# Scores of an attention layer on four row tiles: a head's 96 stacked rows cut into three pieces of 32

## The reference

```python
qkv = x @ Wqkv                                   # 16 heads of 16 features
q, k = apply_rope(q), apply_rope(k)
q = q / jnp.sqrt(jnp.sum(q * q, -1, keepdims=True) + 1e-06)   # k likewise
attn = jax.nn.softmax(jnp.einsum('bthd,bshd->bhts', q, k) / math.sqrt(HD), axis=-1)
out = jnp.einsum('bhts,bshd->bthd', attn, v).reshape(b, t, d) @ Wo + bo
x = _layernorm(x + out)
```

## Time and profile before

| what | us |
|---|---|
| median of 3 runs | 1380.87 |
| the profiled execution | 1376.04 |
| its span, first to last instruction | 1374.0 |
| TensorE busy / ScalarE busy / VectorE busy in the span | 1256.9 / 915.8 / 793.3 |

### The profile page before, as it was taken

One profiled execution on the slowest core, in us unless ns is written; L12 is line 12 of the kernel. 1 busy time (PEld: TensorE's weight loads), 2 busy tenths in 40 slices (PEclk: granted clock), 3 DMA queues, 4 the chain that ended last, 5 costly groups with the idle time before them and its releaser, 6 DMA issues. The chain is left out here.

```text
span 1374.0 us, 20853 instructions
## 1 busy us (share of the span) xinstructions
PE 1256.9 (91%) x7142; PEld 674.2 (49%) x7142; DVE 793.3 (58%) x1815; ACT 915.8 (67%) x1617; POOL 323.5 (24%) x246
## 2 busy tenths in 40 slices
PE   4699999999998898999999999999982899999996
PEld 2233343343343333444444444444332799999986
DVE  5236456456451777787878787878744234443432
ACT  1588878878876575676766666666661477776765
POOL 3113332332331111022222222222123012212211
PEclk8899999999999899999999999999996899999998
DMA  5173243243243121214131313131349211111110
GB/s 180 64 170 105 72 139 98 71 141 95 73 137 108 47 90 50 79 47 109 47 109 47 109 47 109 48 93 47 126 153 311 71 56 51 54 56 51 58 52 15
DMA packets 101485, 123.11 MB, mean 90 GB/s; under 512 B 7234, under 2 KB 87234, under 8 KB 101379
## 3 DMA queue, kind: packets, MB, share of 16 engines
q1 hardware_dynamic: 76534, 83.35, 19.6%
q10 hardware_dynamic: 20416, 25.56, 5.9%
q0 software_dynamic: 4432, 12.87, 3.1%
HBM read 47.41 MB, written 24.27 MB: 52 GB/s over the span
## 5 line engine op out<-in xcount | busy, mean ns | idle before, releaser
L692 ACT ACTIVATE w_space<-bank 128x512 f32<-128x512 f32 x1024 | 561.7, 606 | 277.7 <-PE bank L472 263.6
L886 DVE TENSOR_REDUCE negm<-bank 128x1 f32<-128x512 f32 x512 | 334.3, 685 | 97.9 <-PE bank L504 94.4
L472 PE MATMUL bank<-w_space 96*128 96x512 bf16 (+1 forms) x1024 | 355.1, 385 | 26.5 <-DMA w_space<-work_space 14.2
L489 PE MATMUL bank<-w_space 128*32 128x512 f32 x2048 | 275.3, 610 | 0.2 <-ACT w_space L701 0.2
L472 PEld LDWEIGHTS bank<-w_space 96*128 96x128 bf16 (+1 forms) x1024 | 93.5, 99 | 303.7 <-ACT w_space L692 217.3
L504 PE MATMUL bank<-w_space 96*128 96x512 bf16 x512 | 197.5, 386 | 18.1 <-DVE negm L886 8.8
L666 PE MATMUL bank<-w_space,work_space 128*128 x624 | 141.2, 380 | 0.0
L535 PE MATMUL bank<-work_space,wqkv_sb 128*128 128x512 f32 x256 | 125.0, 613 | 9.5 <-DMA wqkv_sb<-in_w_qkv_dram 6.4
L1245 POOL TENSOR_TENSOR work_space<-w_space,work_space 128x1024 bf16<-128x1024 f32 x32 | 68.3, 2133 | 266.3 <-ACT work_space L742 146.5
L666 PEld LDWEIGHTS bank<-w_space,work_space 128*128 128x128 f32 x624 | 115.6, 190 | 14.3
L1300 POOL DMA_INDIRECT out_dram<-rows_sb,work_space x39 | 59.8, 1533 | 241.9 <-DVE rows_sb L1197 241.9
(11 more groups left out here) (130 smaller groups left out, 1414.3 us busy)
## 6 DMA issues: line engine op xcount, KB each, us to landing
w_space<-work_space SPq DMA_DIRECT2D x372, 128.0 KB
w_space<-in_w_dram SPq DMA_DIRECT2D x10, 1024.0 KB, 14.2
work_space<-rows_dram SPq DMA_DIRECT2D x39, 256.5 KB, 2.6
w_space<-in_w_dram ACTq DMA_DIRECT2D x6, 1024.0 KB, 6.3
work_space<-in_x_t_dram ACTq DMA_DIRECT2D x8, 512.0 KB, 3.7
work_space<-in_x_dram ACTq DMA_DIRECT2D x8, 512.0 KB
x_dram<-xo SPq DMA_DIRECT2D x16, 256.0 KB, 4.2
h_dram<-row_sb SPq DMA_DIRECT2D x16, 256.0 KB, 2.2
```

Source lines behind the costliest of these rows:

```text
L472: nc.tensor.matmul(bank[:, :], k_stack[0:rows, b % 2, HEADS_AT_ONCE * g + j, kt * P:(kt + 1) * P], q_stack[0:rows, b % 2, HEADS_AT_ONCE * ...
L489: last = nc.tensor.matmul(pv_bank[VW * j:VW * (j + 1), :], v_aug[:, b % 2, at:at + VW], probs[:, q % PROBS, j, :], start=(kt == 0), stop=( ...
L692: nc.scalar.activation(probs[:, q % PROBS, j, :], st_bank(b, c)[0][:, :], ACT.Exp, scale=SCALE).then_inc(exps, 1)
L886: ve.tensor_reduce(negm[:, c % TT, c // TT:c // TT + 1], mx_ring.bank(b, (g, c))[:, :], axis=AX.X, op=ALU.max, negate=True).then_inc(mx_ri ...
```

## The change

In the first layer the stack of a head becomes three pieces of 32 rows. The 32 rows of head j of a group lie on partitions 32j to 32j + 31, so four heads fill 128 partitions, and piece `part` of group g stands at place 4g + part of the free dimension. `score_quad` makes the scores of all four heads at the head of a quad (chunk 0): three passes, in each one matmul of 32 rows per head, the four heads on four row tiles and into four banks, and the three passes add up in the bank. The first pass of each head waits for its bank; each head's last pass counts its score. The weights' columns, the rotation tables and the matrix that sums squares are laid out so that the stack's DMAs (same number and bytes) write 32 partitions x 4 places in place of 8 partitions x 16 places.

Scores of the first layer use five banks (0 to 3 and 7) until quad 10 of batch 7 (`ALL_BANKS`), then three; there the fourth head waits for the first head's exponential and goes alone. `o_ring` keeps bank 5 alone. The row of ones moves from the first loads to two loads on SP behind the k copies of units 8 and 9, as the first layer now uses all partitions. Some tasks of the first layer move: on VectorE aq, ak, uk, hk and lk (ak now after hq), on TensorE nk by one chunk, and on ScalarE sq, sk, nq, nk, TP0, TP1, R1 and R2 to places behind the fourth exponential of a quad, the copy of oT too (`COPY_AFTER` 3). The second layer's scores are made as before.

```diff
+ALL_BANKS = CHUNKS * LAST_A + HEADS_AT_ONCE * (QUADS - MAX_LEAD)
...
-    dict(qA=(0, 3), qB=(1, 2), kA=(2, 3), kB=(3, 3), sq=(3, 3), aq=(4, 3), nq=(6, 0), sk=(6, 1),
-         uq=(7, 1), ak=(7, 2), hq=(7, 2), lq=(8, 0), nk=(8, 2), uk=(9, 2), hk=(9, 3), lk=(10, 1),
+    dict(qA=(0, 3), qB=(1, 2), kA=(2, 3), kB=(3, 3), sq=(3, 3), aq=(5, 0), nq=(6, 0), sk=(6, 1),
+         uq=(7, 1), hq=(7, 2), ak=(8, 0), lq=(8, 0), nk=(8, 3), uk=(10, 1), hk=(10, 2), lk=(11, 0),
...
-ACT_LAG = (dict(other=1),
+ACT_LAG = (dict(sq=4, nq=3, sk=6, nk=4, TP0=3, TP1=4, R1=2, R2=2, other=1),
...
-COPY_AFTER = (1, 2)
+COPY_AFTER = (3, 2)
...
-        st_banks, mx_banks, pv_bank = psum[0:4], (psum[3], psum[7]), psum[6]
+        st_banks, mx_banks, pv_bank = psum[0:4] + psum[7:8], (psum[3], psum[7]), psum[6]
...
-        o_ring = Ring("out", [psum[5], psum[7]], sem)
+        o_ring = Ring("out", [psum[5]], sem)
...
-            if b < LAST_A:
-                return st_banks[c % 4], CHUNKS * b + c - 3
-            return st_banks[(CHUNKS * (b - LAST_A) + c) % 3], CHUNKS * b + c - 2
+            n = CHUNKS * b + c
+            if n < ALL_BANKS:
+                return st_banks[n % 5], n - 4
+            return st_banks[(n - ALL_BANKS) % 3], n - 2
...
+        def slot_of(stack, b, slot, half):
+
+            at = 2 * slot + half
+            if second(b):
+                return stack[at:STACK:ROW_STEP, b % 2, :, :]
+            return stack[at % 4:P:4, b % 2, slot // 2:H:4, :]
...
+            def score_quad(b, q):
+
+                g, kt = q // TT, q % TT
+                if q == 0:
+                    for arrived in stack_in:
+                        pe.wait_ge(arrived, 16 * STACK_DMAS * (b + 1))
+                own = [st_bank(b, HEADS_AT_ONCE * q + j) for j in range(HEADS_AT_ONCE)]
+                banks = len({id(bank) for bank, _ in own})
+                for heads in (range(banks), range(banks, HEADS_AT_ONCE)):
+                    for part in range(3):
+                        at = 4 * g + part
+                        for j in heads:
+                            bank, read = own[j]
+                            if part == 0:
+                                wait(pe, exps, read)
+                            rows = slice(32 * j, 32 * j + 32)
+                            last = nc.tensor.matmul(bank[:, :],
+                                                    k_stack[rows, b % 2, at, kt * P:(kt + 1) * P],
+                                                    q_stack[rows, b % 2, at, :],
+                                                    start=(part == 0), stop=(part == 2))
+                            if part == 2:
+                                last.then_inc(scores, 1)
...
-                        pe.wait_ge(exps, CHUNKS * LAST_A)
-                        pe.wait_ge(o_ring.drained[1], o_ring.used[1])
+                        pe.wait_ge(exps, ALL_BANKS)
...
-                        if attended is not None:
+                        if attended is not None and second(attended):
                             score(attended, HEADS_AT_ONCE * q + j)
+                        elif attended is not None and j == 0:
+                            score_quad(attended, q)
...
-                (w1_space[STACK:STACK + NEG, H * T:2 * H * T], ones_pairs))
...
+                    if qk and b in (BATCH, BATCH + 1):
+                        at = H * T + b % 2 * (H * T // 2)
+                        sp.dma_start(w1_space[STACK:STACK + NEG, at:at + H * T // 2],
+                                     ones_pairs[:, 0:H * T // 2]).then_inc(ones_in, 16)
```

More of the change, by code:

```diff
@@ L318, in program @@
         neg_in = sem("neg_in")
+        ones_in = sem("ones_in")
         x_in = [sem("x_in0"), sem("x_in1")]
@@ L347, in program @@
         h_out = [sem("h_out0"), sem("h_out1")]
[L348 to L351 removed]
+        N_FIRST, N_LATER, N_CONST_OPS = 5, 12, 3
+        st_banks, mx_banks, pv_bank = psum[0:4] + psum[7:8], (psum[3], psum[7]), psum[6]
         p_ring = Ring("proj", [psum[i] for i in (4, 0, 1, 2, 3, 5, 6, 7)], sem)
[L353 removed]
+        o_ring = Ring("out", [psum[5]], sem)
         mx_ring = Ring("max", mx_banks, sem)
@@ L361, in program @@
                         elif name[:2] in OUT_BANK:
-                            o_ring.add(b, name, len(o_ring.uses) % 2 if n <= LAST_A else 0)
+                            o_ring.add(b, name, 0)
         for b in range(BATCH, 2 * BATCH):
@@ L440, in stack_copies @@
                     for half in range(2 if slots[slot] == part else 0):
-                        eng.dma_start(stack[2 * slot + half:STACK:ROW_STEP, b % 2, :, :],
+                        eng.dma_start(slot_of(stack, b, slot, half),
                                       parts[:, qk, part, half, :]).then_inc(stack_in[qk], 16)
@@ L467, in score @@
                         pe.wait_ge(arrived, 16 * STACK_DMAS * (b + 1))
+                if second(b) and c == 0:
+                    pe.wait_ge(ones_in, 16 * min(b - BATCH + 1, 2))
                 if second(b) and j == 0 and kt == 0:
@@ L1326, in _ @@
                 (gate_w_sb[:, 0, :], gate_w[0:P, :]), (gate_w_sb[:, 1, :], gate_w[P:D, :]),
-                (gate_b_sb[:, :], gate_b.partition_broadcast(P)),
-                (w1_space[STACK:STACK + NEG, H * T:2 * H * T], ones_pairs))
+                (gate_b_sb[:, :], gate_b.partition_broadcast(P)))
             assert (len(first), len(later)) == (N_FIRST, N_LATER)
@@ L1387, in lay_out, with columns @@
     a = {k.removeprefix("L0_"): np.asarray(v) for k, v in inputs.items()}
-    def columns(w):
-        qk = w[:, :2 * D].reshape(D, 2, H, 2, HALF).transpose(0, 1, 3, 4, 2).reshape(D, 2 * D)
+    def columns(w, second):
+        qk = w[:, :2 * D].reshape(D, 2, GROUPS, HEADS_AT_ONCE, 2, HALF)
+        qk = qk.transpose((0, 1, 4, 5, 2, 3) if second else (0, 1, 4, 3, 5, 2)).reshape(D, 2 * D)
         return np.ascontiguousarray(np.concatenate([qk, w[:, 2 * D:]], axis=1))
@@ L1393, in lay_out @@
     angles = (np.arange(T, dtype=np.float32)[None, :] * inv_freq.astype(np.float32)[:, None])
-    table = lambda f: np.repeat(f(angles).astype(np.float32), H, axis=0)
-    of_head = np.arange(P) % H
+    head_rows = np.arange(P).reshape(HEADS_AT_ONCE, HALF, GROUPS)
+    of_half = ((head_rows // GROUPS) % HALF).reshape(P)
+    table = lambda f: f(angles).astype(np.float32)[of_half]
+    of_head = (head_rows % GROUPS * HEADS_AT_ONCE + head_rows // (P // HEADS_AT_ONCE)).reshape(P)
     return {
-        "x": a["attn_x"], "x_t": a["attn_x"].transpose(0, 2, 1), "w_qkv1": columns(a["attn_Wqkv"]), "w_o1": a["attn_Wo"],
+        "x": a["attn_x"], "x_t": a["attn_x"].transpose(0, 2, 1), "w_qkv1": columns(a["attn_Wqkv"], False), "w_o1": a["attn_Wo"],
         "b_o": a["attn_bo"], "ln1_w": a["ffn_ln1_w"], "ln1_b": a["ffn_ln1_b"],
-        "w_qkv2": columns(a["ffn_w_qkv"]), "w_o2": a["ffn_w_proj"], "ln2_w": a["ffn_ln2_w"],
+        "w_qkv2": columns(a["ffn_w_qkv"], True), "w_o2": a["ffn_w_proj"], "ln2_w": a["ffn_ln2_w"],
         "ln2_b": a["ffn_ln2_b"], "gate_w": a["ffn_gate_w"], "gate_b": a["ffn_gate_b"],
```

## The result

The changed kernel takes **1395.18 us** (median of 4 runs, 1393.39 to 1395.96); the kernel before took 1380.36 beside it on the same chip. The ratio is 1.0107, with a 95% interval of 1.0095 to 1.0119: slower by 1.1%, 2 us from the forecast. The profiled execution took 1395.14 (span 1393.2).

A forecast was written before the change was run, and what follows sets the result against it. TensorE was taken as the bound (busy 50.05 of a 51.37 us stage), ScalarE some 10 behind. Stages +7.4, start +1.5 and batch 7 +3 made +11.9 us: 1387.9 from the profiled execution, 1393 on the median; range 1367 to 1410.

The forecast's parts named there:

- long quads: First-layer quads with an output projection: from 3.70 to 3.60 us each, eight of them giving back 0.8 a stage.
- Scores: A quad's scores: four matmuls of 0.22 (0.88) become three rounds taken at 0.72, lower end 0.65, upper end 1.16.
- The rival that weights don't overlap: Weight loads run one behind the other: a quad's scores take 1.16, not 0.72, kernel 1442 us; chance 0.06.
- Drains: Each change between row tiles, column tiles and full width costs 0.09; 15 extra a stage, 1.35 us.
- The fourth head: Head 3 waits for the previous quad's third exponential: quad 13 +0.56, quads 11 and 15 together +0.24.
- the prediction's signs: What would show it right, including TensorE waiting for exponentials at the head of quads 5, 6, 13 and 15.
- Quads 4 to 8: ScalarE has no hole, TO0 waits for TP1's copy in the one out bank: 15.79 against 14.63, +1.16.
- A stage: One steady first-layer stage: -0.80 + 0.56 + 0.24 + 1.16, less about 0.1, so +1.05; seven stages +7.4 us.
- Start: Before the first score: hq's four operations now stand ahead of the k sum, bounds 0 and 2, taken +1.5 us.
- nothing, if they land as fast: k copies cost nothing if 32 partitions land as fast as 8; otherwise lateness falls on the next stage's first score.
- Batch 7: Last six quads have three banks, head 3 waits and runs alone: +1.34 each, 8.0 at most, taken +3 us.
- The clock rival: Two standstills a stage could halve the clock for 3.4 us over quad 8: +1.5 a stage, 1403 us; chance 0.04.

The follow-up runs named there:

- order2: Changed kernel with TP0 and TP1 moved to quads 3 and 4 and the k half normalised a quad sooner: 1384.17 us, ratio 1.0049.
- order3: order2 with VectorE adding k's squares ahead of TO0's division: 1382.38 us, ratio 1.0030.
- order5: order3 with VectorE splitting the k half behind the sum of WO0 instead of ahead of it: 1377.39 us, ratio 1.0002.

## Why the prediction was right

The forecast (slower, 1393) held, and so did the mechanism of the stages: TensorE waits for ScalarE in quads 4 to 8 and 14, and long quads gain next to nothing. The stage's loss was twice what the sum has, though, the start had the wrong sign and batch 8 was left out, and that the total came out 2 us off is in good part luck.

- **Scores.** Rounds start 0.226 and 0.216 apart (records of quad 10: 287.162, 287.388, 287.604); with the drain 0.76, where 0.72 + 0.09 was taken: the lower end. The rival that weights don't overlap is out by the 0.34 for twelve loads.
- **Drains: the step that was mis-sized.** A change between row and column tiles costs 0.10 (0.66 + 0.10 = 0.76), near the 0.09 taken. A projection behind the product with v costs more: 1.92 up to the next score, where 1.73 + 0.09 = 1.82 was forecast. The first two of L615's eight matmuls stand 0.320 apart, the others 0.216. I read the 0.10 as a full-width load (0.19) that nothing hides: the first two loads start only 0.108 apart, the second ends 0.03 ahead of the second matmul, and every later one lies under the matmul ahead of it. Before, a score stood between product and projection, the loads started with it, and the first two matmuls stood 0.220 apart. So the seven long quads other than quad 14 gave back 0.04 in all (forecast 0.7). The Trainium skill (TensorEngine Tiling (Array Packing), Key Properties) has a change of tiling mode drain TensorE; the trace agrees, at 0.09 to 0.10 a change.
- **The fourth head.** Quads 13 and 14 together went from 5.66 to 6.15, +0.49; forecast 0.56 - 0.10. The wait stands at the head of quad 14, not of 13 as the prediction's signs have it, since it is the quad behind a short one that waits. Quads 11 and 15 together grew by 0.09, not 0.24: quad 11 shrank by 0.06, and the 0.15 of quad 15 come from ScalarE's wait for VectorE shown above (2.34 in order2).
- **Quads 4 to 8.** The mechanism as told: TP1's copy at 12.03 after the start of quad 4 (forecast 11.86), TO0 at 12.71 (12.53), the end at 16.11 (15.79): +1.48 for +1.16. TensorE stood 1.63 longer over quad 6's scores and 1.64 ahead of TO0.
- **A stage** so comes to +2.03, not +1.05: 0.66 of the difference comes from the seven long quads (0.13 of it a wait of quad 12's fourth head, the rest mainly the loads behind drains), 0.32 from quads 4 to 8; the other terms cancel. The k copies cost nothing, as forecast: no first score of these stages waits for a DMA.
- **Start: wrong in sign.** -3.2 for +1.5. The first score came at 40.87, not 44.06, its wait for the copies 7.88 instead of 14.22. The copies of both kernels begin at 25.3. From their first packet to the end of the last they take 15.1 with row tiles in nine of the ten profiles (13.8 with the old order) and 17.9 to 18.5 in the four profiles of the layout of before, under either order. So the 32-partition copies land sooner; "nothing, if they land as fast" left out that they could be faster.
- **Batch 7** +2.2 for +3, but the clock is in it (0.91 before, 0.93 after), so that the term was right isn't shown. **Batch 8** was no term: +4.9. Of that 1.72 lies in its quads 5 and 7 and comes with the order (0.49 and 1.23 also in the run with the new order alone; the 1.23 is gone where TP1's copy comes earlier), and 3.2 in the quads with the two stretches at half clock shown above, which the kernel before doesn't have. In the 10 us ahead of the one at 539.60 TensorE never stood for more than 0.94. Why the grant fell there stays open.
- **The clock rival** didn't come in this kernel, whose standstills were 1.6; it did in batches 2 to 5 of the run with 96 rows and the new order, behind standstills of 1.91, and not in its batches 1 and 6 with the same standstill.
- **The sum.** +11.9 was forecast, and the two profiled executions differ by 19.1: seven stages 7.6 and batch 8 4.9 more than the sum has, start 4.7 and batch 7 0.8 less. The medians differ by 14.8, since the profiled execution of before was 4.3 below its median and that of after was at its own.

**What the change cost, then:** with the scores at the head of the quad row tiles and 96 rows come out nearly even in a steady stage (51.63 against 51.48 in one order), the fifth score bank is worth 1.4 a stage more than a second out bank, and most of a stage's loss was the order of ScalarE's and VectorE's work (53.40 to 51.63, 1.77 of 2.03).

## What to carry to other kernels

A matmul form that saves its own time can give it back at its borders: count what the instruction between two tilings was hiding, and when the first result of a batched group comes out. Moving the scores to the head of the quad changes what every other engine must finish first, so an order of work has to be found anew with it; the order alone moved this kernel by 1.8% with row tiles (1.0179 to 1.0002) and by 1.4% with 96 rows (1.0129 to 0.9988, part of it the clock). A wait removed at one place can come back at the next reader of a single buffer, when that reader stands on the same queue, as WO0's sum did in order3.

## What the runs showed of the hardware that was not expected

VectorE's product of two tiles (L954), 0.68 alone, takes 1.47 when it starts while GpSimd's subtraction (L1281) runs. It ends 0.546 to 0.549 after GpSimd does in each of seven stages of order2, order3 and order5, whether it had started 0.22 ahead of GpSimd's end (order2, 0.77 long) or 0.85 to 0.92 ahead of it. It stands until GpSimd is done rather than running slower. The Trainium skill (SBUF — State Buffer, SBUF: two separate sides) says so: a port pair shared by the two is an exclusive lock, and the loser blocks. In order3 this took back what the earlier addition had gained on that queue: the product started 0.66 sooner than in order2 (277.00, 277.66) and ended when it had.

The twelve loads of a quad's row tiles, 0.09 each, lengthen its rounds by 0.01 in all (rounds start 0.226 and 0.216 apart, full-width matmuls 0.216). Copies to 32 partitions moved the first stage's 3.15 MB in 15.1 us instead of 18.2 to 8 partitions (profiles of after and before), in the same 3072 packets of 1 KB.
